# A fused audio tower on one core: the order of the window attention's step on TensorE and DVE, and the engine of one bias copy

## What is computed

```python
def _sliding_window_attn(q, k, v):        # offsets -32 to 32
    s = jnp.einsum('bhsd,bhsd->bhs', q, k_sh) * scale   # for each offset
    p = jax.nn.softmax(scores, axis=-1)
    out = out + p[..., idx:idx + 1] * jnp.roll(v, -o, axis=2)
...
qkv = (x @ W_qkv + b_qkv).reshape(B, S, 3, HEADS, HD)
attn = _sliding_window_attn(q, k, v)
return attn @ W_proj + b_proj
...
h = h + _L0_attn_ref(_layernorm(h, axis=-1), ...)
h = h + _L0_ffn_ref(_layernorm(h, axis=-1), ...)
```

## Time and profile before

| what | us |
|---|---|
| median of 3 runs | 544.42 (542.15 to 547.11) |
| the profiled execution | 544.12 |
| its span | 541.9 |
| mean granted clock of TensorE | 0.951 of full speed |
| PE busy | 493.9 (91%) |
| DVE busy | 414.6 (77%) |
| ACT busy | 356.4 (66%) |
| POOL busy | 333.1 (61%) |

### The profile page before, as it was taken

How to read it: one execution, slowest core, us unless ns; L and a number is a source line. 1 busy time by engine, 2 the same in 40 slices (tenths; PEclk the granted TensorE clock), 3 DMA queues, 4 the chain that set the end, 5 groups by cost and what they waited for, 6 DMA issues and landing times.

```text
span 541.9 us, 13950 instructions
## 1 busy us (share of the span) xinstructions
PE 493.9 (91%) x4554; PEld 350.7 (65%) x4554; DVE 414.6 (77%) x1726; ACT 356.4 (66%) x1066; POOL 333.1 (61%) x373
## 2 busy tenths in 40 slices
PE   6998999999997689999999999998798999999973
PEld 4777676666664467667667776656466666666642
DVE  3797678888884466878878787865669999999972
ACT  5985578898886354544554444455568888888850
POOL 2860668787875567766766776664325565655544
PEclk9999589999999599999999999999889999999995
DMA  5540212222222100000000000000000000000000
GB/s 166 152 151 16 62 40 62 61 62 58 58 62 63 35 23 21 19 22 31 27 21 20 20 20 20 1 1 1 0 3 9 14 21 20 21 2 21 22 19 21
DMA packets 21945, 19.88 MB, mean 37 GB/s; under 512 B 14210, under 2 KB 18466, under 8 KB 21746
## 3 DMA queue, kind: packets, MB, share of 16 engines
q1 hardware_dynamic: 21298, 18.28, 11.6%
q10 hardware_dynamic: 576, 0.71, 0.4%
HBM read 16.81 MB, written 2.18 MB: 35 GB/s over the span
## 4 chain that ended last, share of the span: by engine, by line
PE 49%; DVE 9%; ACT 4%; issue 3%; POOL 2%; ACTq 0%; POOLq 0%; DVEq 0%
PE quad L801 10%; PE quad L778 9%; PE bank L823 6%; DVE wprobsT L1231 4%; PE bank L882 3%; PE bank L853 3%; PE quad L770 3%; PE bank L901 3%; PE bank L870 2%; PE bank L889 2%; PE bank L862 2%; ACT woT L1007 2%; PE bank L792 1%; DVE z_all L1236 1%; PE bank L816 1%
## 5 line engine op out<-in xcount | busy, mean ns | idle before, releaser
L476 POOL TENSOR_SCALAR put<-keyb,c 100x1000 f32<-100x1000 bf16 x32 | 89.1, 2784 | 44.2 <-DMA keyb<-key_scratch 26.7
L992 ACT ACTIVATE wprobs<-quad,wmax 125x125 f32<-125x125 f32 x256 | 72.2, 378 | 7.6 <-DVE wmax L1207 7.6
L609 ACT ACTIVATE probs<-quad,negmax 100x250 f32<-100x250 f32 x128 | 58.4, 468 | 19.8 <-DVE negmax L561 18.7
L1207 DVE CUSTOM_DVE_ANT_0 quad<-quad,c 125x125 f32<-125x125 f32 x256 | 65.0, 317 | 2.1 <-PE quad L846 1.8
L778 PE MATMUL quad<-h1T,w 128*128 128x500 f32 x128 | 62.2, 611 | 0.7 <-ACT hid L964 0.6
L801 PE MATMUL quad<-w,hid 128*125 128x128 f32 x512 | 58.8, 273 | 0.1
L801 PEld LDWEIGHTS quad<-w,hid 128*125 128x125 f32 x512 | 57.3, 188 | 0.8 <-issue 0.5
L491 PE MATMUL bank<-c,probs 100*125 100x100 f32 x256 | 46.8, 309 | 2.3 <-ACT probs L609 1.6
L491 PEld LDWEIGHTS bank<-c,probs 100*125 100x125 f32 x256 | 35.5, 202 | 19.9 <-issue 12.1
L964 ACT ACTIVATE hid<-quad,vec_cols 128x500 f32<-128x500 f32 x64 | 43.0, 676 | 7.7 <-PE quad L778 4.4
L1151 DVE TENSOR_SCALAR n<-t,mv,rstd 125x128 f32<-125x128 f32 x128 | 44.5, 409 | 2.7 <-POOL rstd L1051 1.6
(11 more groups left out here) (132 smaller groups left out, 1245.2 us busy)
## 6 DMA issues: line engine op xcount, KB each, us to landing
keyb<-key_scratch SPq DMA_DIRECT2D x64, 97.7 KB
xa<-xT SPq DMA_DIRECT2D x8, 500.0 KB, 3.5
xt<-xtok SPq DMA_DIRECT2D x16, 250.0 KB
out<-o_all SPq DMA_DIRECT2D x7, 250.0 KB
w<-weights SPq DMA_DIRECT2D x1, 1024.0 KB, 7.1
vec_rows<-rows SPq DMA_DIRECT2D x1, 448.0 KB, 5.1
c<-consts ACTq DMA_DIRECT2D x1, 428.5 KB, 6.6
w<-weights ACTq DMA_DIRECT2D x1, 192.0 KB, 3.7
```

The costliest lines, as they stand in the source:

```text
L476: nc.gpsimd.tensor_scalar(put[u % 3][:, :, :], keyb[p][:, :, :], c[0:ROWS, CONST["sidx"]], None, ALU.is_equal).then_inc(put_done, 1)
L609: nc.scalar.activation(probs[p][:, ch, :], s_bank[ch][0:ROWS, 0:L], ACT.Exp, bias=negmax[p][:, ch:ch + 1], accum_out=rowsum[p][:, ch:ch + ...
L992: nc.scalar.activation(probs[p][:, j, :], s_of(j), ACT.Exp, bias=negmax[p][:, j:j + 1], scale=-1.0).then_inc(exp_done, 1)
L1207: nc.vector.tensor_tensor_reduce(s_of(j), s_of(j), c[0:LH, CONST["band"]], 1.0, OFF, ALU.add, ALU.min, negmax[p][:, j:j + 1]).then_inc(min ...
```

## The change

In `window`, on three engines:

- TensorE: PV and OFT move ahead of QK, and PJ moves ahead of P0.
- DVE: oF is gone; Z moves ahead of C0. The split of the minima in two calls changes no instruction.
- ACT: oF is new, after e5 and ahead of e6, as an activation (Identity with a bias column), the same form as kT's. In step 1, where all exponentials are in one piece, there is none (it starts with step 3).

Each moved instruction has the same waits as before.

```diff
@@ TensorE
-                if part in (None, "qkv") and within(u, -2, B - 2):
-                    ...
-                    ins.then_inc(qk_ready, 1)
-
                 if part in (None, "qkv") and within(u, 2, B + 2):
                     wait(pe, otok_done, u - 2)
...
                     ins.then_inc(pv_ready, 1)
 
+                if part in (None, "qkv") and within(u, 3, B + 3):
+                    pe.wait_ge(otok_done, u - 2)
+                    nc.tensor.transpose(y_of, otok[:, :], ident[0:LH, 0:LH]).then_inc(oF_ready, 1)
+
+                if part in (None, "qkv") and within(u, -2, B - 2):
+                    ...
+                    ins.then_inc(qk_ready, 1)
+
                 if part in (None, "qkv") and within(u, -1, B - 1):
                     ...
-                if part in (None, "qkv") and within(u, 3, B + 3):
-                    pe.wait_ge(otok_done, u - 2)
-                    nc.tensor.transpose(y_of, otok[:, :], ident[0:LH, 0:LH]).then_inc(oF_ready, 1)
+                if part in (None, "early") and within(u, 3, B + 3):
+                    pe.wait_ge(oF_done, u - 2)
+                    nc.tensor.matmul(y_proj, oF[:, :], w[:, WEIGHT["wp"]], start=True, stop=True).then_inc(proj_ready, 1)
 
                 if part in (None, "early") and within(u, 0, B):
                     pe.wait_ge(exp_done, H * u + 4)
...
                     ins.then_inc(pT0_ready, 1)
-
-                if part in (None, "early") and within(u, 3, B + 3):
-                    pe.wait_ge(oF_done, u - 2)
-                    nc.tensor.matmul(y_proj, oF[:, :], w[:, WEIGHT["wp"]], start=True, stop=True).then_inc(proj_ready, 1)
@@ ACT
                 if part in (None, "exps") and within(u, 0, B) and u != 1:
-                    exponents(2, 8)
+                    exponents(2, 6)
+                if part in (None, "exps") and within(u, 3, B + 3):
+                    act.wait_ge(oF_ready, u - 2)
+                    wait(act, proj_ready, u - 3)
+                    nc.scalar.activation(oF[:, :], y_of, ACT.Identity, bias=col("wv_b")).then_inc(oF_done, 1)
+                if part in (None, "exps") and within(u, 0, B) and u != 1:
+                    exponents(6, 8)
@@ DVE
-                    mask_and_min(2, 8)
-                if part in (None, "rest") and within(u, 3, B + 3):
-                    dve.wait_ge(oF_ready, b + 1)
-                    wait(dve, proj_ready, b)
-                    nc.vector.tensor_scalar(oF[:, :], y_of, col("wv_b"), None, ALU.add).then_inc(oF_done, 1)
-                if part in (None, "rest") and within(u, 0, B):
-                    ...
-                    nc.vector.tensor_copy(probsT[p][:, 0:4, :].rearrange("p h l -> p (h l)"), t_bank[0][0:LH, 0:4 * LH]).then_inc(pT0_done, 1)
+                    mask_and_min(2, 6)
+                if part in (None, "minima") and within(u, 0, B):
+                    mask_and_min(6, 8)
                 if part in (None, "rest") and within(u, 3, B + 3):
                     dve.wait_ge(proj_ready, b + 1)
...
                     nc.vector.tensor_tensor(z_all[:, b:b + 1, :], y_proj.unsqueeze(1), z_all[:, b:b + 1, :], ALU.add).then_inc(z_done, 1)
+                if part in (None, "rest") and within(u, 0, B):
+                    ...
+                    nc.vector.tensor_copy(probsT[p][:, 0:4, :].rearrange("p h l -> p (h l)"), t_bank[0][0:LH, 0:4 * LH]).then_inc(pT0_done, 1)
                 if part in (None, "rest") and within(u, 3, B + 3):
                     dve.wait_ge(z_done, b + 1)
```

More of the change, by code:

```diff
@@ L884, in window @@
                     ins.then_inc(pv_ready, 1)
+                if part in (None, "qkv") and within(u, 3, B + 3):
+                    pe.wait_ge(otok_done, u - 2)
+                    nc.tensor.transpose(y_of, otok[:, :], ident[0:LH, 0:LH]).then_inc(oF_ready, 1)
+                if part in (None, "qkv") and within(u, -2, B - 2):
+                    wait(pe, qT_done, u + 2)
+                    wait(pe, v_done, u + 1)
+                    pe.wait_ge(n3T_done, (u + 2) // 2 + 1)
+                    for dst, name in ((x_k, "wk"), (x_q, "wq")):
+                        ins = nc.tensor.matmul(dst, w[:, WEIGHT[name]], n3T_all[:, LH * (u + 2):LH * (u + 2) + LH], start=True, stop=True)
+                    ins.then_inc(qk_ready, 1)
                 if part in (None, "qkv") and within(u, -1, B - 1):
@@ L1222, in window @@
                 if part in (None, "minima") and within(u, 0, B):
-                    mask_and_min(2, 8)
-                if part in (None, "rest") and within(u, 3, B + 3):
-                    dve.wait_ge(oF_ready, b + 1)
-                    wait(dve, proj_ready, b)
-                    nc.vector.tensor_scalar(oF[:, :], y_of, col("wv_b"), None, ALU.add).then_inc(oF_done, 1)
-                if part in (None, "rest") and within(u, 0, B):
-                    dve.wait_ge(pT0_ready, u + 1)
-                    wait(dve, pv_ready, u - 1)
-                    nc.vector.tensor_copy(probsT[p][:, 0:4, :].rearrange("p h l -> p (h l)"), t_bank[0][0:LH, 0:4 * LH]).then_inc(pT0_done, 1)
+                    mask_and_min(2, 6)
+                if part in (None, "minima") and within(u, 0, B):
+                    mask_and_min(6, 8)
                 if part in (None, "rest") and within(u, 3, B + 3):
@@ L1236, in window @@
                     nc.vector.tensor_tensor(z_all[:, b:b + 1, :], y_proj.unsqueeze(1), z_all[:, b:b + 1, :], ALU.add).then_inc(z_done, 1)
+                if part in (None, "rest") and within(u, 0, B):
+                    dve.wait_ge(pT0_ready, u + 1)
+                    wait(dve, pv_ready, u - 1)
+                    nc.vector.tensor_copy(probsT[p][:, 0:4, :].rearrange("p h l -> p (h l)"), t_bank[0][0:LH, 0:4 * LH]).then_inc(pT0_done, 1)
                 if part in (None, "rest") and within(u, 3, B + 3):
```

## The result

The changed kernel takes 558.76 us (median of 4 runs, 555.89 to 562.47), the kernel before 543.43 beside it (542.15 to 547.11). The ratio is 1.0269, with a 95% interval of 1.023 to 1.0308: slower, by some 15 us. Forecast was 559.6. The four executions lie 6.6 us apart.

A forecast was written before the change was run, and what follows sets the result against it. The old bound was a T-to-oT ring across PE, DVE and ACT; the new one runs through oF, PJ and P0. 28 steps by 0.54 are 15.1 us, 15.3 with the tail: 559.4, as median 559.6, range 553.5 to 564.5.

The forecast's parts named there:

- The ring: Changed step's loop m0, e0, C1, e2 to e5, oF, PJ, P0, C0, bs, ag, m0: 4.88 us against 4.34.
- The step: From one m0 to the next: 4.88 us, longer by 0.54; 4.82 or 5.06 with oF at its bounds.
- PV ahead of QK costs nothing by itself: On PE, PV waits for otok; no cost as long as PJ isn't wanted before 2.58 us after m0.
- PE's new wait: On PE ahead of PV, a wait for otok of about 0.6 to 0.8 us.
- PJ ahead of P0, where I saw the loss: On PE, P0 could run from 2.58 us after m0 but stands behind PJ and oF until 3.22.
- C0 waits for P0: On DVE, a sign: C0 waits for P0 and starts 0.64 us after it, at 3.86 after m0.
- The tail and the start: Outside the 28 steps: tail 0.06 us more, thrice; start nothing, 0.5 either way at most.
- Faster by DVE's relief: Rival: oF off DVE and T's wait gone make the step 4.00, total 534.9 us; chance 0.03.
- ACT's stream as the bound: Rival where it cancels out: ACT's stream gives a step of 4.15 or some 4.25, total 541.6 us; chance 0.04.
- PE's ring without oF: Rival where only the PV and QK swap counts: step 4.56, total 550.3 us; chance 0.07.
- The clock: Rival: new gaps drop PE to 1.2 GHz for part of the stage, total 581 us; chance 0.05.
- The sum: Whole kernel: 15.3 us more, 544.1 to 559.4 for the profiled execution, 559.6 as a median.

The follow-up runs named there:

- e5: Not a run: one of the exponentials on ACT; the changed kernel has oF right after it.
- e6: Not a run: one of the exponentials on ACT; the changed kernel has oF right ahead of it.
- e0: Not a run: the first of the exponentials on ACT, ahead of C1.
- e2: Not a run: one of the exponentials on ACT, the first behind C1 in the changed kernel.
- e3: Not a run, and not named in the kept text: the exponential on ACT behind e2, for which P0 waits.
- e4: Not a run, and not named in the kept text: the exponential on ACT between e3 and e5.
- e7: Not a run, and not named in the kept text: the last exponential on ACT, behind e6.
- second: Kernel before with only oF moved to ACT, between e5 and e6, both orders as before; 544.08 us, ratio 1.0.
- fourth run: Changed kernel with oF two exponentials earlier on ACT, between e3 and e4; 543.88 us, ratio 0.9996.
- fifth run: Changed kernel with QK put back ahead of PV and OFT on TensorE; 558.16 us, ratio 1.0245.
- third run: Kernel before with only PV and OFT moved ahead of QK on TensorE; 551.42 us, ratio 1.0128.
- ninth run: Changed kernel with only P0 put back ahead of PJ on TensorE, Z still ahead of C0; 555.05 us, ratio 1.0165.
- tenth: Changed kernel with oF back on DVE, behind m7 and ahead of Z, new orders kept; 556.38 us, ratio 1.0198.
- twelfth run: Eighth run's kernel with oF moved from DVE to ACT, between e5 and e6; 542.31 us, ratio 0.9958.
- eleventh run: Kernel before with V alone moved behind P0 on TensorE; 541.04 us, ratio 0.9932.
- fourteenth: The fourth run's kernel: changed kernel with oF between e3 and e4; 543.88 us, ratio 0.9996.
- eighth run: Kernel before with V behind P0, C1 behind e2, reciprocal and otok behind m2, oF still on DVE; 536.23 us, ratio 0.9862.
- first run: Changed kernel with P0 again ahead of PJ and C0 again ahead of Z, oF still on ACT; 551.95 us, ratio 1.0138.

## Why the prediction was right

The ring was the right one, and its terms, in the order in which the prediction went round (forecast, then measured in the timelines above), are:

| from, to | forecast | measured |
|---|---|---|
| m0, e0 | 0.45 | 0.42 |
| e0, C1 | 0.51 | 0.51 |
| C1, e2 | 0.48 | 0.47 |
| e2, oF | 1.00 | 0.99 |
| oF, PJ | 0.46 | 0.46 |
| PJ, P0 | 0.32 | 0.32 |
| P0, C0 | 0.64 | 0.64 |
| C0, bs | 0.59 | 0.59 |
| bs, ag | 0.33 | 0.32 |
| ag, m0 | 0.10 | 0.10 |
| step | 4.88 | 4.82 |

- *The step.* 0.06 too long, half of it in m0 to e0, which I had taken from step 3, where m0 took 0.30 and not 0.27. oF took 0.41, as kT's row said. The estimate of 0.38 from the Trainium skill ("ScalarE: Activation LUTs", section "What ACT_TABLE_LOAD costs") was further off in this kernel; in the second and fourth run oF took 0.37.
- *PV ahead of QK costs nothing by itself.* Right in the changed kernel (fifth run), and only there: alone it costs 0.22 (third run). The forecast called PE's new wait about 0.6 to 0.8; it is 0.58.
- *PJ ahead of P0, where I saw the loss.* Right, with one thing left out: P0 alone put back ahead of PJ recovers 0.23 (ninth run), but not because C0 is then free; Z, put ahead of C0, keeps oF on the ring. By the waits each of the two moves on its own holds C0 behind oF; PJ ahead of P0 without Z ahead of C0 was not run.
- *C0 waits for P0.* Partly. On DVE the idle time is ahead of Z (0.93), and from Z's end to C0 only some 0.15 is left.
- *The tail and the start.* I counted 0.2 and nothing. The part behind m0 of step 31 became 0.3 shorter (22.05 to 21.79). In the two profiles the start of the window attention differs by 1.8 before any moved instruction has run (first S at 376.1 and 374.3), and by 1.4 at m0 of step 3; in both the granted clock is 0.50 from 394 to 397, just ahead of that.
- *The rivals.* Faster by DVE's relief: refuted by the second, tenth and twelfth run. With it falls, for this kernel, the advice of the Trainium skill that moving work from a saturated DVE to Scalar may make sense ("Perfetto Trace Analysis", section "Optimizing Scalar/DVE Operations"). DVE was the fullest engine, busy for 28.45 of 30 us, and not what the step waited for. ACT's stream as the bound: not here, but it is the ring in the twelfth run, at 4.24, and the forecast for it had said 4.15 to 4.25. PE's ring without oF: 4.56 forecast for oF early; the fourth run has 4.33, the miss explained there. The clock: 1.00 from 398 to the end of the stage, so it did not fall in the new gaps.
- *The sum.* Forecast for the profiled execution 559.4, measured 555.9. Of the 3.5 between (the parts are rounded), 1.3 are the step (28 steps, one of them longer, below), 1.4 the start, 0.5 the tail and 0.4 the time around the span. The median lies 0.8 below the 559.6 forecast. That closeness is partly luck: the executions lie 6.6 apart, and the error in the step alone is 1.3 over the stage.

## What to carry to other kernels

Where hand-ordered engines pass a piece of work round, write the ring out, with each instruction's start from the last one's, and ask of every moved instruction which chain now stands in front of it in its queue: here a projection that only the output needs was put ahead of a transpose that the next step needs, and tied the two chains together. Busy shares don't show this: oF was taken from DVE, as full as any other engine or fuller, in three settings (the second kernel, the twelfth, and the changed kernel beside the tenth), and in none did the step get shorter. The gain was in a filler (V) that stood ahead of an urgent instruction (P0) and could as well stand behind it (0.08 a step, eleventh run), and in the moves of C1 and otok beside it (0.11 together, not told apart). Where a view of the chain puts an instruction down to its own queue after an idle time of a few hundredths, compare its distance from the other things it waits for between kernels: Z to oT was 0.40 in thirteen kernels, and only the fourteenth showed what the queue alone takes.

## What the runs showed of the hardware

- The distance from one TensorE instruction group to the next depends on what is around it: V to the next is 0.32 when OFT follows, and 0.22 when PJ follows in the fourth and eighth run, or P0 in the first; PJ to P0 is 0.32 behind a wait for oF and 0.27 without one. A row taken from one neighbourhood was off by up to 0.1 us in another.
- In each of the nine kernels that have oF on ACT, e0 of step 29 starts 0.70 to 0.74 after its m0 and not 0.42 to 0.45, and in none of the five that have it on DVE. In eight of the nine the step from 29 to 30 is 0.19 to 0.28 longer for it; in the first run's, whose ring doesn't go through e0, it is 4.57 like the others. In the changed kernel (5.10 in place of 4.82; m0 at 522.38):

```profile
523.08 0.62 ACT L992 ACTIVATE wprobs<-quad,wmax 125x125 f32<-125x125 f32 x2 [1.20 <-DVE wmax L1213]
```

The idle time is 1.20 where it is 0.92 in the other steps of this kernel. What holds it was not tried.
- The step of a kernel is the same to 0.01 in its steady steps, but for that one and one other in some of the profiles, and shorter or longer at the stage's two ends, while m0 of step 3 stands anywhere from 396.0 to 403.0 us in the profiles of all the kernels. In these profiles most of the scatter comes from ahead of the window attention, so a step read from one profile told apart what the times alone needed several runs for.
